# Softplus of the step size by one ScalarE function between two table loads, in a fused AdaLN, state-space and expert kernel

## The reference, cut to what matters

```python
x_dbl = jnp.einsum('bld,ed->ble', u, W_x)
dt_raw = x_dbl[..., :dt_rank]            # and B_sel, C_sel
dt = jax.nn.softplus(jnp.einsum('blr,dr->bld', dt_raw, W_dt) + b_dt)
A_bar = jnp.exp(dt[..., None] * A)       # A = -exp(A_log), 16 states
dB_u = (dt * u)[..., None] * B_sel[:, :, None, :]
_, h = jax.lax.associative_scan(_combine, (A_bar, dB_u), axis=1)
y = jnp.einsum('bldn,bln->bld', h, C_sel)
```

## Time and profile before

| what | value |
|---|---|
| median of 3 runs | 1218.32 us (1218.26 to 1220.63) |
| span of the profiled execution, first to last instruction | 1214.9 us |
| VectorE busy | 1023.8 us, 84% |
| GpSimd busy | 1001.4 us, 82% |
| TensorE busy (matmul) | 932.1 us, 77% |
| ScalarE busy | 715.2 us, 59% |
| DMA queue q1 | 41.2% of 16 engines' span |
| mean granted TensorE clock | 0.881 |

### The profile page before, as it was taken

One profiled execution on the slowest core, in us unless ns is written; L12 is line 12 of the kernel. 1 busy time (PEld: TensorE's weight loads), 2 busy tenths in 40 slices (PEclk: granted clock), 3 DMA queues, 4 the chain that ended last, 5 costly groups with the idle time before them and its releaser, 6 DMA issues. The chain is left out here.

```text
span 1214.9 us, 13519 instructions
## 1 busy us (share of the span) xinstructions
PE 932.1 (77%) x4235; PEld 590.9 (49%) x4235; DVE 1023.8 (84%) x826; ACT 715.2 (59%) x1412; POOL 1001.4 (82%) x357
## 2 busy tenths in 40 slices
PE   5335444578878888698877898788968897789998
PEld 4101111245644556455554565355644565456786
DVE  2399999999899989998999989998999989995110
ACT  4864569556874669557865588466955367331200
POOL 1376676689997999799997999799979999797453
PEclk9656766599998998999998999898998999889899
DMA  5607160364427171555346261727144443611132
GB/s 164 155 19 168 40 138 1 89 173 101 125 70 208 46 190 36 135 145 134 92 104 175 65 169 46 171 91 182 52 114 132 113 115 84 166 45 47 57 100 61
DMA packets 90552, 131.21 MB, mean 108 GB/s; under 512 B 13536, under 2 KB 73512, under 8 KB 90480
## 3 DMA queue, kind: packets, MB, share of 16 engines
q1 hardware_dynamic: 90480, 130.34, 41.2%
HBM read 54.50 MB, written 8.65 MB: 52 GB/s over the span
## 5 line engine op out<-in xcount | busy, mean ns | idle before, releaser
L965 POOL TENSOR_TENSOR h<-h,Cr 128x2048 f32<-128x2048 f32 x129 | 582.4, 4517 | 97.0 <-DVE h L835 53.5
L835 DVE TENSOR_TENSOR_SCAN h<-av,ps 128x1024 f32<-128x1024 f32 x256 | 584.7, 2284 | 16.6 <-DVE ps L828 0.9
L588 PE MATMUL ps<-xg,we 128*128 128x256 f32 x2048 | 501.1, 401 | 21.3 <-POOL xg L1002 18.9
L588 PEld LDWEIGHTS ps<-xg,we 128*128 128x128 f32 x2048 | 402.0, 201 | 119.1 <-POOL xg L1002 33.8
L1002 POOL TENSOR_TENSOR xg<-h2T,gbc 128x1024 f32<-128x1024 f32 x128 | 304.3, 2383 | 64.8 <-DMA gbc<-gates 30.7
L828 DVE TENSOR_TENSOR ps<-ps,dd 128x1024 f32<-128x1024 f32 x256 | 315.4, 1232 | 46.7 <-PE ps L473 26.1
L631 ACT ACTIVATE av<-dd,An 128x1024 f32<-128x1024 f32 x256 | 289.5, 1141 | 69.7 <-DVE h L835 50.9
L492 PE MATMUL ps<-h,gam 128*32 128x512 f32 x1024 | 141.2, 674 | 44.1 <-POOL h L965 33.4
L685 ACT ACTIVATE Cr<-ps 128x512 f32<-128x512 f32 x64 | 38.0, 596 | 99.8 <-PE ps L533 79.9
L473 PE MATMUL ps<-S,sel 64*128 64x512 f32 x128 | 51.7, 487 | 48.3 <-DVE ps L828 48.3
L492 PEld LDWEIGHTS ps<-h,gam 128*32 128x32 f32 x1024 | 29.2, 117 | 119.8 <-issue 77.4
(11 more groups left out here) (100 smaller groups left out, 855.9 us busy)
## 6 DMA issues: line engine op xcount, KB each, us to landing
dd<-src SPq DMA_DIRECT2D x512, 128.0 KB, 2.4
gbc<-gates SPq DMA_DIRECT2D x128, 256.0 KB, 3.7
X<-in_x SPq DMA_DIRECT2D x8, 1024.0 KB, 8.2
out<-X SPq DMA_DIRECT2D x32, 256.0 KB, 3.3
XN<-in_x SPq DMA_DIRECT2D x7, 1024.0 KB, 7.9
we<-in_We SPq DMA_DIRECT2D x2, 1024.0 KB, 8.7
XN<-in_x SPq DMA_DIRECT2D x2, 512.0 KB, 5.2
Cr<-in_wmod SPq DMA_DIRECT2D x1, 1024.0 KB, 5.3
```

Source lines behind the costliest of these rows:

```text
L588: e = pe.matmul(bk[:, m * 256:(m + 1) * 256], we[:, hf, 2 * ep + e2, m * P:(m + 1) * P], xg[:, i % XG, e2, hf], start=(ep == e2 == m == hf ...
L835: dve.tensor_tensor_scan(h[:, u % HS], av[:, u % AS], wide(BP), 0.0, ALU.mult, ALU.add).then_inc(s_scan, 1)
L965: pool.tensor_tensor(hu, hu, Cr[:, q:q + 1].to_broadcast([P, n, L]), ALU.mult).then_inc(s_ch, n)
```

## The change

The function Softplus stands in another of ScalarE's tables than exp and ln, which all other steps use. Now ScalarE reads each piece of the raw step size once, with its bias, into `src`; when both pieces of a half are there, the new step `sp` loads the Softplus table, applies the function in place to the whole half, and loads the exp and ln table back. The first half of the first batch is done straight from PSUM, piece by piece, between its two loads. VectorE's `corr` and GpSimd's first two operations are gone, and five semaphores with them. `XM`, which shared memory with the temporary `sp_t`, has its own now, and the waits for that sharing are gone. Nearly all of the 161 offsets of `AT` are new; two lines of them stand here.

```diff
-          ldx=29.86, gam=19.72, dl0=20.66, dl1=36.03, dls=3.26, rdl=0.66, corr=0.19, dt=7.52, C=25.68, CS=2.8,
+          ldx=32.64, gam=23.95, dl0=21.19, dl1=35.9, dls=3.41, rdl=0.42, sp=0.81, dt=7.88, C=25.58, CS=3.73, Cc=0.43,
...
-            put(s + AT["corr"], "corr", b, hf, c)
-            put(s + AT["dt"], "dt", b, hf, c)
+            if in_bank(b, hf):
+                put(s + AT["dt"], "dt", b, hf, c)
+        if not in_bank(b, hf):
+            put(s + AT["sp"], "sp", b, hf)
+            put(s + AT["dt"], "dt", b, hf)
...
+def in_bank(b, hf):
+
+    return b == hf == 0
...
+        def positive(eng, b, hf, halves=(0, 1)):
+
+            if in_bank(b, hf):
+                for c in halves:
+                    emptied(eng, ("dl", b, hf, c))
+            else:
+                eng.wait_ge(s_dt, 2 * b + hf)
...
-                    act.activation(sp_t[:, 0], mb(s), ACT.Abs, bias=bd[:, hf:hf + 1]).then_inc(s_abs, 1)
-                    if c == 0 and i:
+                    cs = slice(c * CH, (c + 1) * CH)
+                    if in_bank(b, hf):
+                        if c == 0:
+                            act.preload_act_table_set("softplus")
+                        done(act, s)
+                        release(act.activation(src[:, 0, cs], mb(s), ACT.Softplus, bias=bd[:, hf:hf + 1]), s)
+                        if c == 1:
+                            act.preload_act_table_set("natural_log_exp_and_others")
+                        return
...
-                    act.activation(src[:, 0, cs], mb(s), ACT.Relu, bias=bd[:, hf:hf + 1]).then_inc(s_abs, 1)
-                    act.wait_ge(s_abs, 2 * i + 2)
-                    act.activation(mb(s), sp_t[:, 0], ACT.Exp, scale=-1.0).then_inc(s_e, 1)
-                    if i:
-                        act.wait_ge(s_lp, i)
-                    act.wait_ge(s_e, i + 1)
-                    act.activation(sp_t[:, 1], mb(s), ACT.Identity, bias=1.0).then_inc(s_up, 1)
-                    act.activation(src[:, 1, cs], mb(s), ACT.Ln, bias=1.0).then_inc(s_l, 1)
+                        act.wait_ge(s_dtu, 2 * b + hf + 1)
+                    done(act, s)
+                    release(act.activation(src[:, 0, cs], mb(s), ACT.Identity, bias=bd[:, hf:hf + 1]), s)
...
+            def soft_plus(b, hf):
+
+                for c in range(2):
+                    emptied(act, ("dl", b, hf, c))
+                act.preload_act_table_set("softplus")
+                act.activation(src[:, 0], src[:, 0], ACT.Softplus).then_inc(s_dt, 1)
+                act.preload_act_table_set("natural_log_exp_and_others")
...
-                    pool.tensor_tensor(src[:, 1, cs], src[:, 1, cs], sp_t[:, 1], ALU.subtract).then_inc(s_lp, 1)
...
-                    pool.tensor_tensor(src[:, 0, cs], src[:, 1, cs], src[:, 0, cs], ALU.add).then_inc(s_dt, n)
```

More of the change, by code:

```diff
@@ new lines @@
+AT = dict(exp=0.54, mul=0.01, scan=0.63, ch=7.93, Bs=0.65, y=7.82, stat0=-2.76, stat0s=0.51, rstd0=1.18,
+          rsb0=1.81, xh0=3.8, xh0s=0.11, xT0=15.7, xT0h=0.2, xTs=2.34, rxT0=0.49, wx=4.41, rwx=1.05, S=-0.67,
+          ldx=32.64, gam=23.95, dl0=21.19, dl1=35.9, dls=3.41, rdl=0.42, sp=0.81, dt=7.88, C=25.58, CS=3.73, Cc=0.43,
+          rC=0.41, ddt=36.97, ddts=1.8, ddu=38.28, ddus=1.66, zs=2.91, ldx2=33.26, z=5.19, zX=-0.95, zd=1.46,
+          stat1=6.82, stat1s=0.35, rstd1=9.58, rsb1=1.28, xh1=11.03, xh1s=0.13, xh1g=0.57, xT1=11.33, xT1h=0.1,
+          xT1s=1.69, rxT1=0.49, lg=13.56, rlg=0.43, lT=0.9, soft=0.42, softe=0.68, top=0.96, gT=1.78, rgT=0.81,
+          gw=11.28, gr=27.35, xg=23.26, xgs=1.78, gl=-2.22, f=-3.09, fE=0.44, o=2.08, oX=1.54, out=12.44, md1=-53.75,
+          gates=-31.95, ga=-0.84, bn0=-124.93, bn0s=14.46, stat1A=5.1, stat1B=8.15, stat1sA=-6.79, stat1sB=2.89,
+          rstd1A=5.94, rstd1B=7.94, rsb1A=0.8, rsb1B=5.29, xh1A=6.94, xh1B=44.04, xh1sA=0.05, xh1sB=0.52, xh1gA=32.69,
+          xh1gB=7.73, xT1A=8.49, xT1B=25.75, xT1hA=0.3, xT1hB=14.96, xT1sA=-14.82, xT1sB=20.11, rxT1A=0.67,
+          rxT1B=21.87, lgA=10.48, lgB=76.86, rlgA=-0.73, rlgB=-12.46, lTA=0.61, lTB=9.53, softA=2.37, softB=-17.86,
+          softeA=-2.63, softeB=13.91, topA=3.4, topB=12.37, gTA=2.2, gTB=24.56, rgTA=1.12, rgTB=-6.82, gwA=19.4,
+          gwB=21.58, grA=41.8, grB=129.45, xgA=34.06, xgB=170.36, xgsA=9.76, xgsB=4.14, glA=-6.88, glB=27.59,
+          fA=36.59, fB=-17.53, fEA=56.16, fEB=41.0, oA=17.27, oB=56.62, oXA=-10.56, oXB=49.64, outA=36.63, outB=88.88,
+          stat1P=6.73, stat1sP=0.35, rstd1P=9.22, rsb1P=0.47, xh1P=10.68, xh1sP=0.28, xh1gP=0.49, xT1P=11.51,
+          xT1hP=1.09, xT1sP=1.15, rxT1P=0.53, lgP=14.05, rlgP=0.42, lTP=0.39, softP=-0.4, softeP=1.08, topP=-0.09,
+          gTP=0.88, rgTP=0.32, gwP=10.57, grP=26.74, xgP=21.39, xgsP=1.83, glP=-3.86, fP=-3.24, fEP=0.6, oP=5.09,
+          oXP=8.79, outP=57.86)
@@ L402, in _ @@
                     _, H, j = s
-                    sp.wait_ge(s_dt, 2 * H + 2)
+                    positive(sp, *divmod(H, 2))
                     if H:
@@ L409, in _ @@
                     _, H, j = s
-                    sp.wait_ge(s_dtu, 2 * H + 2)
+                    sp.wait_ge(s_dtu, H + 2)
                     if H:
@@ L701, in _ @@
                     decay(s[1])
+                elif s[0] == "sp":
+                    soft_plus(s[1], s[2])
                 elif s[0] == "read":
@@ L970, in _ @@
                 elif s[0] == "dt":
-                    _, b, hf, c = s
-                    cs, i = slice(c * CH, (c + 1) * CH), 4 * b + 2 * hf + c
-                    emptied(pool, ("dl", b, hf, c))
-                    pool.tensor_tensor(src[:, 1, cs], src[:, 1, cs], sp_t[:, 1], ALU.subtract).then_inc(s_lp, 1)
-                    if b and c == 0:
-                        continue
-                    n = 2 if b else 1
-                    cs = slice((c + 1 - n) * CH, (c + 1) * CH)
-                    pool.wait_ge(s_lp, i + 1)
-                    pool.tensor_tensor(src[:, 0, cs], src[:, 1, cs], src[:, 0, cs], ALU.add).then_inc(s_dt, n)
-                    pool.wait_ge(s_dt, i + 1)
-                    for p in range(c + 1 - n, c + 1):
-                        emptied(pool, ("xT", 0, b, p, hf))
-                    pool.tensor_tensor(src[:, 1, cs], src[:, 0, cs], hT[:, b % 2, hf, cs], ALU.mult).then_inc(s_dtu, n)
+                    b, hf = s[1:3]
+                    H, halves = 2 * b + hf, s[3:] or (0, 1)
+                    cs = slice(halves[0] * CH, (halves[-1] + 1) * CH)
+                    positive(pool, b, hf, halves)
+                    if H:
+                        for j in range(NJ):
+                            pool.wait_ge(s_ddu[j], 64 * H)
+                    for c in halves:
+                        emptied(pool, ("xT", 0, b, c, hf))
+                    pool.tensor_tensor(src[:, 1, cs], src[:, 0, cs], hT[:, b % 2, hf, cs], ALU.mult).then_inc(s_dtu, 1)
                 elif s[0] == "gam":
```

37 lines of the change are left out of this document (2 added, 35 removed).

## The result

The changed kernel takes **1199.61 us** (median of 4 runs, 1198.99 to 1200.66), the kernel before beside it 1218.29 (4 runs, 1217.23 to 1220.63). The ratio is **0.9834, 95% interval 0.9812 to 0.9857**: faster, by 18.7 us between these two medians and by 20 us by the ratio. The forecast was 1184, with 1175 to 1200 as its range: the direction held, the outer range held by 0.4 us, the likeliest case (1176 to 1191) did not.

The account below looks back on a forecast made before the run. The prediction took VectorE's chain of product, scan, product as the bound; gains 12.6 + 14.0 + 6.6 + 1.0 = 34.2 us cut the 1214.9 us span to 1180.7, and 3.4 around it gave 1184 us, range 1175 to 1200.

Parts of the forecast that it names:

- the likeliest case: Whole kernel: all gains come as summed, 1184 us, from 1176 to 1191; chance 0.57.
- rival B: VectorE's stream: waits for TensorE's spread of B stay or others their size replace them; gain 20, 1198 us, chance 0.19.
- The bound: Scan stream: VectorE's chain of product, scan, product bounds the kernel, 3.64 us a unit plus its queue's other work.
- VectorE's correction: VectorE's stream: removing 30 corrections between first and last scan saves 0.42 us each, 12.6 us.
- GpSimd's two operations: Batch starts: GpSimd's product ends sooner, removing 14.0 of VectorE's 16.0 us of waits for TensorE's spread of B.
- ScalarE's blocks: ScalarE, each half: two table loads and Softplus, 3.7 us in one block, cost nothing on the path.
- the lead of the `av` ring: ScalarE's exponentials: ready up to 7.5 us before their scans, hiding each block with at least 1.2 us to spare.
- Case C: ScalarE's table switches: each costs twice its load's row, making second halves late; gain 26, 1192 us, chance 0.14.
- Duration of a load: ScalarE's table loads: 1.28 us each, with 2.57 as upper bound; Softplus taken as 1.14.
- Start: Up to the fourth scan: it starts at 58.8 instead of 65.36 us, saving 6.6; bounds 4.3 and 7.2.
- End: After the last scan, where TensorE works off the experts: about 1.0 us saved; bounds -2 and 4.
- Around the span: Outside the profiled span: 3.4 us, the median's excess over the 1214.9 us span, added to the forecast span.

Follow-up runs that it names:

- e5: The changed kernel run again without any edit, on the same chip as the kernel before: 1197.85 us, ratio 0.9834 to the kernel before.
- e4: The changed kernel without the 30 table loads of its 15 later blocks, Relu in place of their Softplus: 1187.95 us, ratio 0.9749 to the kernel before.
- e7: The changed kernel with batch 1's input load issued after the first of four groups of gate copies: 1195.49 us, ratio 0.9815 to the kernel before.
- e3: The changed kernel's mechanism with the offsets of the kernel before (`sp` at 0.81): 1195.45 us, ratio 0.9801 to the kernel before.
- e11: The changed kernel with the offsets of before and batch 1's input loaded early among the gate copies: 1189.97 us, ratio 0.9756 to the kernel before.
- e12: The changed kernel with old offsets and early input load, without the 30 later table loads, Relu for their Softplus: 1192.41 us, ratio 0.9785 to the kernel before.
- e8: The changed kernel with three unused matmuls on TensorE ahead of the transposes that wait for `XM`: 1195.54 us, ratio 0.9828 to the kernel before.
- e9: The changed kernel with each second half's loads and Softplus 3.6 units later on ScalarE, behind the layer norm's normalising: 1216.21 us, ratio 0.9990 to the kernel before.
- the halves of the change: Two runs on the kernel before: VectorE's correction left out, 1212.94 us, ratio 0.9939; GpSimd's subtraction and addition cut to one column, 1211.83 us, ratio 0.9937.
- e10: The changed kernel with both tables loaded once more ahead of each of 15 Softplus, 30 more loads: 1216.35 us, ratio 0.9979 to the kernel before.

## Why the prediction was off, step by step

- *By its own sign the forecast was wrong.* It asked for a stream shorter by about 27 us; the stream is shorter by 11.2 (1037.6 to 1026.4). That the time lies in its range, by 0.4 us, is owed to the room left for rival B and not to the sum. Of the other signs, VectorE's busy time fell by 17.2 us (22 forecast), GpSimd's by 77.0 (79), there are 33 loads of 1.28 us, the scans wait 2.0 us for `av` (none), and the fourth scan is at 61.2 (59).
- *The bound.* Right. VectorE's chain sets the stream, and but for the correction no edit moved the stream without its waits by more than 3 us.
- *VectorE's correction, 12.6.* Right in kind, small by 2.2: the first two traces give 14.8, 0.49 us each instead of 0.42, all the kernels of the table 13 to 17.
- *GpSimd's two operations, 14.0.* This step failed as a term of the sum. Its mechanism held at its own places: waits at batch starts fell from 16.0 to 2.5 us. But the step took those waits for all that VectorE would have, and more came up elsewhere: the net is -3.7 in the first pair of traces. With e5's it is +4.4, but that execution was the fastest of its six.
- *ScalarE's blocks, nothing.* This step failed, too; it is the larger known part of the 17.7 us that the waits fall short of the sum. The cover named was the lead of the `av` ring, and that cover held: 2.0 us of waits for `av` in the whole stream. The follower not looked at was TensorE, which needs what ScalarE does *behind* the block (`XM`, the statistics). e4 prices the loads at 10 us on these offsets. That is not the whole of it: without the loads VectorE still waits 10.6 us in e4's stream, where the forecast left 4.5 of the 18.5. What causes those 6 us more is open. Case C named a cost of the loads, with 1192, but through their duration and the exponentials, and the rows contradict both.
- *Duration of a load.* Right: 1283 ns, 33 times, Softplus 1.06. The Trainium skill, page "ScalarE: Activation LUTs", section "What ACT_TABLE_LOAD costs", adds a drain of about 1380 ns to a switch. No row shows it: the Softplus starts 1.30 us after the load of 589.26 does, the next ACTIVATE 1.30 us after that of 591.63, and ahead of the 30 loads of the blocks ScalarE idles 1.0 us in all (0.7 and 0.3).
- *Start, 6.6.* 4.1; the step "the same reads and statistics as before, 10.6 us" overlooked that batch 1's input isn't there so early. With the input there (e7) the fourth scan is at 58.80, as forecast, though by another route: copies to `dd` bound it.
- *End, 1.0.* 2.5. *Around the span, 3.4.* The changed kernel's profiled execution has 1.9 around its span, and so have the other executions, those of the kernel before too (1.7 to 1.9). The rest was the distance of one execution from the median of others, no cost that stays.
- *The offsets.* The forecast gave them no price of their own. e3 against e5 can't tell them apart (0.9801, 0.9834), e11 against e7 says that the old ones are better by about 0.6% with this mechanism, e4 against e12 that this is hardly so without loads (0.9749 and 0.9785; e12 has the early input load besides).
- *Rival B* (the waits stay or are replaced, 1198, chance 0.19) is what happened, in size and largely in kind, though its size is helped by luck: the start's miss of 2.5 us and the gains of 2.2 and 1.5 at the correction and the end nearly cancel. The text behind it, "nearly all places in the order are new", deserved more weight than the argument about GpSimd's distance.

Shown: the path of the blocks' lateness over `XM`, clock and spread of B at one place, in five kernels (changed, e4, e8, e9, e11), that the loads cost 0.9% on the new offsets, and that this price all but goes on the old ones. Only argued: that the same path makes the whole of the 10 us, of which two kinds of place hold 7 to 8, and why the halves of the change don't add up.

## What to carry to other kernels

When work is packed into one block on an engine with slack, ask for each engine what it next needs from *behind* the block, not only whether the critical engine's own input stays ahead. A wait on an engine off the path can come back through the order of its queue and through its clock. And edit one half at a time only to learn mechanisms: here the halves gave 0.6% each, and the whole on the old offsets gave 2.0%. The likely reason, not shown, is that each half alone leaves the other's engine to hold up the stream; the whole also has a shorter start.

## What the runs showed of the hardware that was not expected

- The granted clock of TensorE was 1.00 ahead of 3.2 us without a matmul and 0.50 behind them, and a group of 16 matmuls of 128x512 then took 3.43 us instead of 1.92. Behind 1.90 and 0.67 us of idling it did not fall, in e11 and e4. The idle time alone does not decide it: behind 1.96 us another group of e4 took 2.84 us at 0.66 (transposes at 469.08, sums at 471.74), and behind 2.82 us one of the changed kernel took 1.92 at 1.00 (998.48 and 999.04). What does, these runs don't tell.
- Two profiled executions of the same kernel differed by 8 us of span, with waits of 22.2 and 14.1 us and mean clocks of 0.864 and 0.880, so one trace of each is no measure of a difference of 0.5%.
- A table load on ScalarE took 1283 ns each of 33 times, and what stood ready behind it started 1.28 to 1.30 us after it did, also where three follow each other (e10: loads at 600.82, 602.10 and 603.39, the Softplus at 604.68).
